# Requesting rows and up weights earlier in an expert stage, and moving a subtract from GpSimd to VectorE

## The chip, the cores and the metric

The kernel runs on one core of a Trainium2 chip. Its time is the device time of one execution in microseconds (us). A core has TensorE (PE, with its weight loads as PEld), VectorE (DVE), ScalarE (ACT), GpSimd (POOL) and SyncE (SP), which here only issues DMAs. Each engine runs its own instructions in order; they meet at semaphores.

## The reference, cut to what matters

Four layers of cross attention over 64 sequences of 64 tokens with 128 features. The change is in the last part of the last layer, a mixture of 8 experts in which each of 4096 tokens goes through its best two:

```python
h = _ln(x, ln_g, ln_b)
logits = h @ rw.T + rb
vals, idx = jax.lax.top_k(logits, K)            # K = 2 of E = 8
gates = jax.nn.softmax(vals, axis=-1)
h1 = gelu(einsum('nd,efd->enf', hf, fc1_w) + fc1_b)     # 128 -> 512, "up"
eo = einsum('enf,edf->end', h1, fc2_w) + fc2_b          # 512 -> 128, "down"
mixed = (gathered * gates_f[..., None]).sum(axis=1)
return x + mixed
```

## The kernel before, in words

The program is ten phases, and all five engines meet between them (`meet`, whose wait is line 223). The ninth phase, routing, writes every token's normalized row twice, once for each of its experts, into a table in HBM (`expert_rows`) in which each expert has its own region, and computes a plan: at which row each group starts and which expert it is. The tenth phase, the expert stage, is the one that changes. It works on NG = 23 groups of 512 rows. Group numbers are g or s; a pass is one turn of the loop on an engine.

What one group goes through:

- SyncE loads its rows (`load_rows`, 260 KB, line 1611), the expert's up weights (512 KB, line 1623), its bias (`e_bias`, 2.5 KB, line 1627) and its down weights (512 KB, line 1623). Row number and expert are read from the plan into a register by `value_load` ahead of the DMA. `rows_in` has RB = 6 buffers, so rows(g) wait until `moe_returned` says that group g-6 has landed; `w_up` and `w_down` have two each, so up(g) waits for the up products of group g-2 (`moe_h_done`) and down(g) for the down products of group g-2 (`moe_down_done`).
- TensorE transposes the rows (L1648), ScalarE reads them from PSUM twice (L1682 to `g_T`, L1684 rounded to `x_hi`, which is `sb_qT_hi`), and the rest, `x_lo = g_T - x_hi` (`sb_qT_lo`, `moe_x_split`), is made by GpSimd (L1732).
- TensorE makes four up products of three matmuls each (in `product_in_parts`, L1086), ScalarE applies Gelu (L1691), VectorE rounds to `h_hi` by a cast (L1715) and subtracts for `h_lo` (L1717).
- TensorE makes the down product, twelve matmuls (L1671), ScalarE adds the bias (L1705), TensorE transposes back (L1662), ScalarE scales the rows by the gate into `y_rows` (L1698, two buffers), and GpSimd scatters them to `expert_outs` in HBM with four indirect DMAs of 128 rows (L1739). Each group's four wait until all earlier ones have landed.

TensorE's pass s holds: transposes of group s+1, up products of s, transposes back of s-2, down product of s-1. It waits for `moe_up_loaded` and `moe_x_split` ahead of the up products. GpSimd's pass s holds the subtract of group s+1 and then the scatter of group s-2. `wait_alone` puts a wait on an instruction of its own (L77). When all groups have landed, SyncE loads the results back (L1633), VectorE adds them to X (L1724), and SyncE writes the output (L1637).

Of the kernel before, what the change touches and what calls it, by code (L numbers as in the profile page):

```python
# [34 lines left out]
P = 128  # L35
# [38 lines left out]
def wait_alone(e, sem, value):  # L74

    wait(e, sem, value)
    e.nop(nofuse=True)  # L77
# [34 lines left out]
def build(nc, a, out):  # L112
# [7 lines left out]
    with ctx:  # L120
# [61 lines left out]
        def col(name):  # L182
            at, n = COLS[name]
            return cols[:, at:at + n]
# [182 lines left out]
        def l0_pool(e, c):  # L367
            e.memset(half_power[:, :], -0.5)
            e.memset(zeros[:, :], 0.0)
            e.wait_ge(sem("params_loaded"), 16 * len(loads))  # L370
            for i in range(2):
                e.tensor_copy(twice[:, S * i:S * i + S], ident[0:S, 0:S])
            e.tensor_copy(ident_16[:, :], ident[:, :])
            e.tensor_copy(bv_wide[:, 0], col("sa_bv").to_broadcast([P, P]))
            e.tensor_copy(bv_wide[:, 1], col("ca_bv").to_broadcast([P, P])).then_inc(sem("bv_wide"), 1)
            e.tensor_tensor(bases[:, 0], row("ln11_b"), row("ca1_bo"), ALU.add)
            meet(e, 0)
            e.memset(rel_sb[:, :, 0:1], 0.0).then_inc(sem("l0_rel_pad"), 1)
            e.memset(blank[:, :, 0:D], 0.0)
            e.memset(blank[:, :, D + 1:ROW], 0.0)  # L380
            e.tensor_copy(blank[:, :, D:D + 1].bitcast(U32), ids[:, 2 * NT:].unsqueeze(2)).then_inc(sem("blank_ready"), 1)

            def fetch_expert(k):
                e.dma_start(e_raw[:, :], a["e_W"][bass.ds(k, 1)].rearrange("a p c -> p (a c)"))\
                    .then_inc(sem("expert_loaded"), 16)

            def split_expert(k):
# [12 lines left out]

            def step(k, u, head, front, back):
                if back:
                    (store_expert if u else fetch_expert)(k)
                if head:
                    m = 2 * k + u + 2
                    e.wait_ge(sem(f"l0_mask_loaded{u}"), 16 * (k + 2))
                    wait_alone(e, sem("l0_rows_done"), 4 * (m - 1))
                    e.tensor_scalar(mask_bias[:, u], mask8[:, u], MASKED, None, ALU.mult)\
                        .then_inc(sem("l0_mask_ready"), 1)
                if back:  # L410
                    n = 2 * k + u
                    x_inv_std_pool(e, "l0", n + 1, n, 1)
                if head:
                    m = 2 * k + u + 2
                    wait_alone(e, sem(f"l0_kv_loaded{u}"), 32 * (k + 2))
                    wait_alone(e, sem("l0_context_done"), 8 * (m - 1))
                    e.tensor_copy(kv_tok[:, u], kv_in[:, u]).then_inc(sem("l0_kv_kept"), 1)
                if back and u:
                    wait_alone(e, sem("expert_stored"), 16 * k + 16)
                elif back:  # L420
                    split_expert(k)
            walk(e, NT, step)

        def l0_tensor(e, c):
# [22 lines left out]
            for left, right in ((wqT, wkT), (wqT, rT), (pb_wide, rT), (wvT, wo0)):  # L447
                if left is wvT:
                    e.wait_ge(sem("l0_vo_loaded"), 32)
                for q in range(4):  # L450
# [2 lines left out]
                        h = 4 * q + i  # L453
                        ins = e.matmul(o[:, i * P:(i + 1) * P], left[:, h], right[:, h], start=True, stop=True)
                    ins.then_inc(sem("l0_table_done"), 1)
            e.wait_ge(sem("bv_wide"), 1)
            for i, n in enumerate(("sa", "ca")):
                ins = e.matmul(PS[:, 2, P * i:P * i + P], bv_wide[:, i], w_out[n][:, :], start=True, stop=True)
            ins.then_inc(sem("bases_done"), 1)
            meet(e, 0)  # L460

            def step(k, u, head, front, back):
# [87 lines left out]
        def l0_vector(e, c):  # L550
# [11 lines left out]
            for table in ("QK", "QR", "rel_bias", "VO"):  # L562
                for q in range(4):
# [9 lines left out]
                        ins = e.tensor_copy(to[:, 4 * q:4 * q + 4], product)  # L573
                    ins.then_inc(sem("l0_table_drained"), 1)
                    n += 1
            e.wait_ge(sem("bases_done"), 1)
            for i, bias in enumerate(("sa_bo", "ca_bo")):
                e.tensor_tensor(bases[:, 1 + i], PS[:, 2, P * i:P * i + P], row(bias), ALU.add)
            meet(e, 0)
# [1027 lines left out]
        def moe_sync(e, c):  # L1607
            def load_rows(s):
                wait_alone(e, sem("moe_returned"), 16 * QT * (s - RB + 1))
                r = e.value_load(plan[0:1, 0, s:s + 1], min_val=0, max_val=MAX_ROW)  # L1610
                e.dma_start(rows_in[:, s % RB], expert_rows[bass.ds(r, GROUP)].rearrange("(p t) c -> p t c", p=P))\
                    .then_inc(sem(f"moe_rows_loaded{s % 4}"), 16)
            load_rows(0)
            for s in range(NG):
                if s + 1 < NG:
                    load_rows(s + 1)
                x = e.value_load(plan[0:1, 1, s:s + 1], min_val=0, max_val=NE - 1)
                wait_alone(e, sem("moe_h_done"), FC * (s - 1))
                wait_alone(e, sem("moe_y_kept"), s - BB + 1)
                for i, to in ((0, w_up), (1, w_down)):  # L1620
                    if i:
                        wait_alone(e, sem("moe_down_done"), s - 1)
                    e.dma_start(to[:, s % 2].bitcast(F32).rearrange("p a c -> p (a c)"),
                                expert_halves[bass.ds(2 * x + i, 1)].rearrange("a p c -> p (a c)"))\
                        .then_inc(sem(f"moe_{('up', 'down')[i]}_loaded{s % 2}"), 16)
                    if not i:
                        e.dma_start(e_bias[:, s % BB], a["e_bias"][bass.ds(x, 1)].rearrange("a p c -> p (a c)"))\
                            .then_inc(sem(f"moe_up_loaded{s % 2}"), 16)
            e.wait_ge(sem("moe_returned"), 16 * QT * NG)
            e.wait_ge(sem("moe_down_done"), NG)  # L1630
            for j in range(4):
                for i in range(2):
                    e.dma_start(returned(i, j), expert_outs[bass.ds(i * NTOK + j * NTOK // 4, NTOK // 4)]  # L1633
                                .rearrange("(t p) d -> p t d", p=P)).then_inc(sem(f"moe_rows_loaded{j}"), 16)
            for j in range(4):
                e.wait_ge(sem("moe_mixed"), 2 * j + 2)
                e.dma_start(out.rearrange("(t b) s d -> (b s) t d", b=2)[:, NT // 4 * j:NT // 4 * (j + 1)],  # L1637
                            X[:, NT // 4 * j:NT // 4 * (j + 1)]).then_inc(sem("out_written"), 16)
# [67 lines left out]
                        .then_inc(sem("moe_y_kept"), 1)  # L1706

        def moe_vector(e, c):
            for s in range(NG):
                u = s % 2  # L1710
                if 0 <= s < NG:
                    wait(e, sem("moe_down_done"), s - 1)
                    for f in range(FC):
# [10 lines left out]
                    e.tensor_tensor(xs, xs, returned(i, j), ALU.add).then_inc(sem("moe_mixed"), 1)  # L1724

        def moe_pool(e, c):
            for s in range(-1, NG + 2):
                if s + 1 < NG:
                    g, v = s + 1, (s + 1) % 2
                    e.wait_ge(sem("moe_x_kept"), g + 1)  # L1730
                    wait(e, sem("moe_h_done"), FC * (g - 1))
                    e.tensor_tensor(x_lo[:, v], g_T[:, v], x_hi[:, v].bitcast(F32), ALU.subtract)\  # L1732
                        .then_inc(sem("moe_x_split"), 1)
                if 0 <= s - 2 < NG:
                    g = s - 2
                    e.wait_ge(sem("moe_y_ready"), g + 1)
                    wait_alone(e, sem("moe_returned"), 16 * QT * g)
                    for t in range(QT):
                        e.indirect_dma_start(  # L1739
                            out=expert_outs, out_offset=bass.IndirectOffsetOnAxis(  # L1740
                                ap=rows_in[:, g % RB, t, D:D + 1].bitcast(U32), axis=0),
                            in_=y_rows[:, g % 2, t], in_offset=None).then_inc(sem("moe_returned"), 16)

        L0 = dict(sync=l0_sync, gpsimd=l0_pool, tensor=l0_tensor, vector=l0_vector, scalar=l0_scalar)
        AT = dict(sync=att_sync, gpsimd=att_pool, tensor=att_tensor, vector=att_vector, scalar=att_scalar)
# [138 lines left out]
```

## Time and profile before

| what | value |
|---|---|
| time before, median of 3 runs | 2361.67 us (2355.17 to 2367.89) |
| the profiled execution, its own time | 2362.87 us |
| its span | 2361.0 us, 53547 instructions |
| busy: TensorE, VectorE, ScalarE, GpSimd | 1858.5, 1403.0, 1143.5, 852.5 us |
| expert stage | first DMA issued at 2150.18 us, last scatter issued at 2337.59 us |

The span goes from the first to the last instruction of the profiled execution; all clock times in this text count from its start. Busy times are sums over an engine's instructions, in which waits and the issue of plain DMAs don't count. Matmuls are pipelined, so that a busy TensorE is not one at its peak.

### The profile page before, as it was taken

Reading aid. Unit: us, or ns where it says so; the run is one execution under the profiler, and the core shown is the slowest. Engines: PE = TensorE matmul, PEld = TensorE weight load, DVE = VectorE, ACT = ScalarE, POOL = GpSimd, SP = SyncE. Lnnn points to the kernel's source line nnn. Section 1 sums busy time; section 2 is a strip of 40 time slices with the busy share of each in tenths; the row PEclk is TensorE's granted clock in tenths of the full one; section 3 lists DMA queues with packets and bytes.
Section 4 is the critical chain, followed back from the end, with each engine's and each line's share of the span. In section 5 each row is a group of like instructions: output and inputs, shape, how many; then the busy total and the mean of one; then the engine's idle time right before and its main releaser. Section 6 shows DMA issues by size and latency. Waiting matters only on the chain. (4 is left out here: it accounts for less than half of the span.)

```text
span 2361.0 us, 53547 instructions
## 1 busy us (share of the span) xinstructions
PE 1858.5 (79%) x15946; PEld 1394.0 (59%) x15946; DVE 1403.0 (59%) x4243; ACT 1143.5 (48%) x3419; POOL 852.5 (36%) x1414
## 2 busy tenths in 40 slices
PE   8898998998999877799789977538997886225993
PEld 7666666766767656566566656215665664224772
DVE  3455555545545546487667764786774785224874
ACT  0455455445445543355456643216774774003772
POOL 0112112111112214355456653343442443443774
PEclk6899999999999998899899989668996997556997
DMA  6544444554454530222100000000000000004775
GB/s 167 106 95 108 106 97 96 113 107 97 108 107 90 117 69 0 104 91 92 60 14 16 16 6 0 0 0 1 0 0 11 12 11 10 27 27 129 224 216 168
DMA packets 214228, 166.54 MB, mean 71 GB/s; under 512 B 27216, under 2 KB 188368, under 8 KB 213776
## 3 DMA queue, kind: packets, MB, share of 16 engines
q1 hardware_dynamic: 205584, 142.84, 24.6%
q0 software_dynamic: 8576, 22.88, 2.8%
q8 instruction: 32, 0.52, 0.1%
q14 instruction: 36, 0.29, 0.0%
HBM read 91.92 MB, written 73.76 MB: 70 GB/s over the span
## 5 line engine op out<-in xcount | busy, mean ns | idle before, releaser
L241 POOL TENSOR_SCALAR sb_next_var_eps<-sb_next_moments 128x1 f32<-128x1 f32 (+1 forms) x184 | 43.2, 235 | 697.0 <-DVE sb_next_moments L236 695.8
L634 DVE CUSTOM_DVE_ANT_0 sb_probs<-PS,sb_work 128x128 f32<-128x128 f32 x512 | 113.3, 287 | 303.2 <-DMA sb_work<-rel_scratch 302.1
L788 POOL TENSOR_TENSOR sb_work<-sb_work,sb_cols 128x512 f32<-128x512 f32 x128 | 134.1, 1048 | 318.4 <-ACT sb_work L995 203.4
L682 ACT ACTIVATE sb_probs<-sb_probs,sb_work 128x128 f32<-128x128 f32 x512 | 197.8, 388 | 100.0 <-DVE sb_work L640 100.0
L926 DVE TENSOR_REDUCE sb_work<-PS 128x8 f32<-128x512 f32 x256 | 175.5, 686 | 87.1 <-PE PS L831 85.9
L674 ACT ACTIVATE sb_work<-PS 128x512 f32<-128x512 f32 x128 | 76.4, 597 | 291.5 <-PE PS L532 291.5
L502 PE MATMUL PS<-sb_work,sb_tables 128*128 128x128 f32 x1024 | 143.8, 298 | 64.1 <-ACT sb_work L664 64.1
L809 PE MATMUL PS<-sb_ident,sb_work 128*128 128x128 f32 x1024 | 168.3, 289 | 32.5 <-ACT sb_work L962 27.6
L962 ACT ACTIVATE sb_work<-sb_work 128x512 f32<-128x512 f32 x256 | 161.3, 630 | 59.9 <-DVE sb_work L928 59.2
L928 DVE TENSOR_TENSOR sb_work<-PS,sb_work 128x512 f32<-128x512 f32 x256 | 177.1, 692 | 8.8
L502 PEld LDWEIGHTS PS<-sb_work,sb_tables 128*128 128x128 f32 x1024 | 134.8, 206 | 74.2 <-ACT sb_work L664 70.2
L809 PEld LDWEIGHTS PS<-sb_ident,sb_work 128*128 128x128 f32 x1024 | 116.5, 145 | 69.1 <-ACT sb_work L962 54.5
L852 PE MATMUL PS<-sb_v_ones,sb_work 128*64 128x18 f32 x4096 | 147.3, 215 | 3.8 <-ACT sb_work L968 3.7
L522 PE MATMUL PS<-sb_work 128*128 128x128 f32 x1024 | 149.6, 290 | 0.0
L852 PEld LDWEIGHTS PS<-sb_v_ones,sb_work 128*64 128x64 f32 x4096 | 134.8, 142 | 22.4 <-issue 10.2
L664 ACT ACTIVATE sb_work<-PS,sb_key_bias 128x128 f32<-128x128 f32 x512 | 138.8, 366 | 17.8 <-PE PS L502 17.8
L968 ACT ACTIVATE sb_work<-PS 128x512 f32<-128x512 f32 x256 | 139.8, 595 | 6.1 <-PE PS L809 2.6
L522 PEld LDWEIGHTS PS<-sb_work 128*128 128x128 f32 x1024 | 125.1, 193 | 29.2 <-issue 29.2
L538 PEld LDWEIGHTS PS<-sb_tables,sb_work 128*128 128x128 f32 x1024 | 116.7, 192 | 21.0 <-ACT sb_work L674 21.0
L538 PE MATMUL PS<-sb_tables,sb_work 128*128 128x128 f32 x1024 | 122.5, 278 | 0.0
L245 POOL TENSOR_TENSOR sb_tile_inv_std<-sb_next_var_eps,sb_half_power 128x1 f32 (+3 forms) x184 | 119.0, 647 | 8.7
L623 DVE COPY sb_probsT<-PS 128x512 f32<-128x512 f32 x128 | 84.1, 688 | 61.4 <-PE PS L494 60.4
(272 smaller groups left out, 4357.4 us busy)
## 6 DMA issues: line engine op xcount, KB each, us to landing
rel_scratch<-sb_work SPq DMA_DIRECT2D x64, 516.0 KB, 6.5
sb_work<-rel_scratch SPq DMA_DIRECT2D x64, 512.0 KB, 6.5
expert_rows<-sb_blank SPq DMA_DIRECT2D x36, 520.0 KB, 2.8
sb_w_up<-expert_halves SPq DMA_DIRECT2D x23, 512.0 KB
sb_w_down<-expert_halves SPq DMA_DIRECT2D x23, 512.0 KB
expert_halves<-sb_e_halves POOLq DMA_DIRECT2D x16, 512.0 KB, 8.2
sb_work<-expert_rows SPq DMA_DIRECT2D x23, 260.0 KB
sb_e_raw<-e_W POOLq DMA_DIRECT2D x16, 256.0 KB, 3.0
```

Of the source, the lines that this page charges most:

```text
L502: ins = e.matmul(PS[:, (shift + g) % 2, i * P:i * P + P], QK[:, 4 * g + i], kvT[:, v, 1], start=True, stop=True)
L522: ins = e.matmul(o[:, i * KL:i * KL + KL], qkT[:, b, h:h + 2], kvT[:, v, :, b], start=False, stop=(i == 3), skip_group_check=True)
L538: ins = e.matmul(o[:, 0:D], pkvT[:, h], VO[:, h], start=(h == 0), stop=(h == H - 1))
L664: ins = e.activation(qkT[:, :, h], PS[:, (shift + g) % 2, i * P:i * P + P] .rearrange("p (b q) -> p b q", b=2), ACT.Identity, bias=key_bia ...
L682: ins = e.activation(probs[:, v, b, hp], probs[:, v, b, hp], ACT.Exp, bias=neg_max[:, v, b, hp:hp + 1], scale=SCALE0, accum_out=row_sum[:, ...
L788: e.tensor_tensor(k_masked[:, u], k_sb[:, u].rearrange("p (b k) -> p b k", b=2).unsqueeze(2) .to_broadcast([P, 2, 4, S]), col("place").uns ...
L809: ins = e.transpose(PS[:, 4 + j, i * P:i * P + P], att_probs[:, u, 8 * j + 2 * i:8 * j + 2 * i + 2], ident[:, :])
L852: ins = e.matmul(values[S * b:S * b + S, 2 * i:2 * i + 2], att_probsT[:, i, S * b:S * b + S], v_ones[:, u, b, 2 * i:2 * i + 2], start=True ...
L926: e.tensor_reduce(top, mine, AX.X, ALU.max).then_inc(sem("att_max_ready"), 1)
L928: e.tensor_tensor(by_group(att_probs[:, v])[:, 2 * j:2 * j + 2], mine, top.unsqueeze(3).to_broadcast([P, 2, 4, S]), ALU.subtract)\
L962: e.activation(att_probs[:, v, 8 * j:8 * j + 8], att_probs[:, v, 8 * j:8 * j + 8], ACT.Exp, scale=c["scale"]).then_inc(sem("att_exp_done"), 1)
L968: e.activation(att_probsT[:, 4 * j:4 * j + 4].rearrange("p i q -> p (i q)"), PS[:, 4 + j], ACT.Copy)\
```

## The change

In SyncE's program of the expert stage the order of requests is another: rows are requested three groups ahead of the pass in which the loop stands, and up weights and bias one group. Down weights are requested one group ahead as well, in the last place. The waits in front of each request are those of before, with the number of the group adapted. The expert's number is now read from the plan twice for each group, once for up and once for down. The subtract `x_lo = g_T - x_hi` goes from GpSimd's program to VectorE's, where it stands ahead of the casts of the group before; GpSimd keeps the scatters and the wait ahead of each group of them. In the first phase two semaphores, `bv_wide` and `bases_done`, become one, `bases`.

```diff
-            e.tensor_copy(bv_wide[:, 1], ...).then_inc(sem("bv_wide"), 1)
+            e.tensor_copy(bv_wide[:, 1], ...).then_inc(sem("bases"), 1)
-            e.wait_ge(sem("bv_wide"), 1)
+            e.wait_ge(sem("bases"), 1)
-            ins.then_inc(sem("bases_done"), 1)
+            ins.then_inc(sem("bases"), 1)
-            e.wait_ge(sem("bases_done"), 1)
+            e.wait_ge(sem("bases"), 2)
...
+            def load_weights(s, i):
+                if i == 0:
+                    wait_alone(e, sem("moe_h_done"), FC * (s - 1))
+                    wait_alone(e, sem("moe_y_kept"), s - BB + 1)
+                else:
+                    wait_alone(e, sem("moe_down_done"), s - 1)
+                x = e.value_load(plan[0:1, 1, s:s + 1], min_val=0, max_val=NE - 1)
+                e.dma_start((w_up, w_down)[i][:, s % 2]..., expert_halves[bass.ds(2 * x + i, 1)]...)
+                    .then_inc(sem(f"moe_{('up', 'down')[i]}_loaded{s % 2}"), 16)
+                if i == 0:
+                    e.dma_start(e_bias[:, s % BB], a["e_bias"][bass.ds(x, 1)]...)
+                        .then_inc(sem(f"moe_up_loaded{s % 2}"), 16)
             load_rows(0)
+            load_weights(0, 0)
+            load_rows(1)
+            load_weights(0, 1)
+            load_rows(2)
             for s in range(NG):
                 if s + 1 < NG:
-                    load_rows(s + 1)
-                x = e.value_load(plan[0:1, 1, s:s + 1], min_val=0, max_val=NE - 1)
-                wait_alone(e, sem("moe_h_done"), FC * (s - 1))
-                wait_alone(e, sem("moe_y_kept"), s - BB + 1)
-                for i, to in ((0, w_up), (1, w_down)):
-                    if i:
-                        wait_alone(e, sem("moe_down_done"), s - 1)
-                    e.dma_start(...)            # up, bias, down of group s
+                    load_weights(s + 1, 0)
+                if s + 3 < NG:
+                    load_rows(s + 3)
+                if s + 1 < NG:
+                    load_weights(s + 1, 1)
...
         def moe_vector(e, c):
-            for s in range(NG):
+            for s in range(-1, NG):
                 u = s % 2
+                if s + 1 < NG:
+                    g, v = s + 1, (s + 1) % 2
+                    e.wait_ge(sem("moe_x_kept"), g + 1)
+                    wait(e, sem("moe_h_done"), FC * (g - 1))
+                    e.tensor_tensor(x_lo[:, v], g_T[:, v], x_hi[:, v].bitcast(F32), ALU.subtract)\
+                        .then_inc(sem("moe_x_split"), 1)
                 if 0 <= s < NG:
...
         def moe_pool(e, c):
-            for s in range(-1, NG + 2):
-                if s + 1 < NG:
-                    g, v = s + 1, (s + 1) % 2
-                    e.wait_ge(sem("moe_x_kept"), g + 1)
-                    wait(e, sem("moe_h_done"), FC * (g - 1))
-                    e.tensor_tensor(x_lo[:, v], g_T[:, v], x_hi[:, v].bitcast(F32), ALU.subtract)\
-                        .then_inc(sem("moe_x_split"), 1)
-                if 0 <= s - 2 < NG:
-                    g = s - 2
-                    e.wait_ge(sem("moe_y_ready"), g + 1)
-                    wait_alone(e, sem("moe_returned"), 16 * QT * g)
-                    ...
+            for g in range(NG):
+                e.wait_ge(sem("moe_y_ready"), g + 1)
+                wait_alone(e, sem("moe_returned"), 16 * QT * g)
+                for t in range(QT):
+                    e.indirect_dma_start(...)
```

## Rows read from the trace of the kernel before

**Rows 1.** Busy time by stretches, expert stage: us of PE, PEld, DVE, ACT, POOL; clock; DMA.

```profile
2175.00:2225.00 50.00, 47.06 (x229) 37.67 (x228) 42.73 (x60) 39.92 (x79) 37.06 (x35) 1.00 0.70 222
```

**Rows 2.** Timeline of TensorE, first up product of four passes [idle before, releaser].

```profile
2157.93 0.79 PE L1086 MATMUL PS<-sb_qT_hi,sb_w_up 128*128 128x512 f32 x1 [1.09 <-DMA sb_work<-e_bias]
...
2224.74 0.47 PE L1086 MATMUL PS<-sb_qT_hi,sb_w_up 128*128 128x512 f32 x1 [0.40 <-issue]
...
2232.35 0.47 PE L1086 MATMUL PS<-sb_qT_hi,sb_w_up 128*128 128x512 f32 x1 [0.95 <-DMA sb_work<-e_bias]
...
2312.70 0.47 PE L1086 MATMUL PS<-sb_qT_hi,sb_w_up 128*128 128x512 f32 x1 [0.81 <-issue]
```

**Rows 3.** Timeline of GpSimd: start us, us, line, operation.

```profile
2223.35 1.29 POOL L1732 TENSOR_TENSOR sb_qT_lo<-sb_work,sb_qT_hi 128x512 fp32r<-128x512 f32 x1
2225.49 1.03 POOL L1739 DMA_INDIRECT expert_outs<-sb_work  x1 [0.85 <-issue]
...
2229.47 1.48 POOL L1739 DMA_INDIRECT expert_outs<-sb_work  x1 [0.30 <-issue]
2230.97 1.28 POOL L1732 TENSOR_TENSOR sb_qT_lo<-sb_work,sb_qT_hi 128x512 fp32r<-128x512 f32 x1
2233.01 0.98 POOL L1739 DMA_INDIRECT expert_outs<-sb_work  x1 [0.76 <-issue]
...
2240.53 0.98 POOL L1739 DMA_INDIRECT expert_outs<-sb_work  x1 [1.26 <-issue]
```

**Rows 4.** Groups of instructions from 2175 to 2319 us: count, busy us, mean ns.

```profile
L1739 POOL DMA_INDIRECT expert_outs<-sb_work x80 | 82.0, 1026 | 39.4 <-issue 34.1 <-ACT sb_work L1698 3.8 <-PE PS L1086 1.5
...
L1732 POOL TENSOR_TENSOR sb_qT_lo<-sb_work,sb_qT_hi 128x512 fp32r<-128x512 f32 x19 | 24.5, 1287 | 0.4
```

**Rows 5.** Timeline of GpSimd, first scatter of groups 0, 21 and 22.

```profile
2175.14 1.45 POOL L1739 DMA_INDIRECT expert_outs<-sb_work  x1 [3.15 <-ACT sb_work L1698]
...
2327.06 0.96 POOL L1739 DMA_INDIRECT expert_outs<-sb_work  x1 [2.01 <-issue]
...
2333.80 0.96 POOL L1739 DMA_INDIRECT expert_outs<-sb_work  x1 [2.00 <-issue]
```

**Rows 6.** The chain that ended last, its step at the last scatter.

```profile
2337.59 2.22 DMA expert_outs<-sb_work
```

**Rows 7.** Timeline of ScalarE, the rescaled rows of group 8.

```profile
2228.37 1.13 ACT L1698 ACTIVATE sb_work<-PS,sb_work 128x128 f32<-128x128 f32 x4
```

**Rows 8.** Timeline of VectorE beside and behind GpSimd's subtract.

```profile
2223.01 1.92 DVE L1715 CAST sb_h_hi<-sb_work 128x512 fp32r<-128x512 f32 x1
2224.96 0.69 DVE L1717 TENSOR_TENSOR sb_h_lo<-sb_work,sb_h_hi 128x512 fp32r<-128x512 f32 x1
```

**Rows 9.** Waits of all engines, 2175 to 2319 us: total us, times, longest.

```profile
DVE sb_h_hi L1715 <- ACT sb_work L1691: 17.9, 18, 1.4
```

**Rows 10.** Waits of SyncE's queue, 2160 to 2330 us: total us, times, longest.

```profile
SPq L77 <- DMA expert_outs<-sb_work: 9.4, 17, 1.0
```

**Rows 11.** Timeline of SyncE's DMA issues, start of the stage and one pass.

```profile
2150.18 1.48 SPq L1611 DMA_DIRECT2D sb_work<-expert_rows  x2
2152.82 0.34 SPq L1623 DMA_DIRECT2D sb_w_up<-expert_halves  x1
...
2224.12 0.33 SPq L1623 DMA_DIRECT2D sb_w_down<-expert_halves  x1
2225.54 0.33 SPq L1611 DMA_DIRECT2D sb_work<-expert_rows  x1
2226.78 0.31 SPq L1623 DMA_DIRECT2D sb_w_up<-expert_halves  x1
```

**Rows 12.** Busy time by stretches of 1 us, the last two columns DMA share and GB/s.

```profile
2224.00:2225.00 1.00, 0.60 (x5) 0.40 (x3) 0.97 (x2) 1.00 (x2) 0.64 (x1) 1.00 0.04 12
...
2230.00:2231.00 1.00, 1.00 (x7) 0.78 (x6) 0.97 (x3) 0.00 (x0) 0.98 (x2) 1.00 0.20 78
...
2238.00:2239.00 1.00, 0.99 (x7) 0.62 (x5) 1.00 (x1) 0.41 (x1) 1.00 (x1) 1.00 0.53 186
```

More of the change, by code:

```diff
@@ L374, in l0_pool @@
             e.tensor_copy(bv_wide[:, 0], col("sa_bv").to_broadcast([P, P]))
-            e.tensor_copy(bv_wide[:, 1], col("ca_bv").to_broadcast([P, P])).then_inc(sem("bv_wide"), 1)
+            e.tensor_copy(bv_wide[:, 1], col("ca_bv").to_broadcast([P, P])).then_inc(sem("bases"), 1)
             e.tensor_tensor(bases[:, 0], row("ln11_b"), row("ca1_bo"), ALU.add)
@@ L1612, in load_rows @@
                     .then_inc(sem(f"moe_rows_loaded{s % 4}"), 16)
+            def load_weights(s, i):
[5 more added lines that the diff above has]
+                x = e.value_load(plan[0:1, 1, s:s + 1], min_val=0, max_val=NE - 1)
+                e.dma_start((w_up, w_down)[i][:, s % 2].bitcast(F32).rearrange("p a c -> p (a c)"),
+                            expert_halves[bass.ds(2 * x + i, 1)].rearrange("a p c -> p (a c)"))\
+                    .then_inc(sem(f"moe_{('up', 'down')[i]}_loaded{s % 2}"), 16)
+                if i == 0:
+                    e.dma_start(e_bias[:, s % BB], a["e_bias"][bass.ds(x, 1)].rearrange("a p c -> p (a c)"))\
+                        .then_inc(sem(f"moe_up_loaded{s % 2}"), 16)
             load_rows(0)
+            load_weights(0, 0)
+            load_rows(1)
+            load_weights(0, 1)
+            load_rows(2)
             for s in range(NG):
                 if s + 1 < NG:
-                    load_rows(s + 1)
-                x = e.value_load(plan[0:1, 1, s:s + 1], min_val=0, max_val=NE - 1)
-                wait_alone(e, sem("moe_h_done"), FC * (s - 1))
-                wait_alone(e, sem("moe_y_kept"), s - BB + 1)
-                for i, to in ((0, w_up), (1, w_down)):
-                    if i:
-                        wait_alone(e, sem("moe_down_done"), s - 1)
[L1623 to L1628, printed above, removed]
+                    load_weights(s + 1, 0)
[3 more added lines that the diff above has]
+                    load_weights(s + 1, 1)
             e.wait_ge(sem("moe_returned"), 16 * QT * NG)
@@ L1726, in moe_pool @@
         def moe_pool(e, c):
-            for s in range(-1, NG + 2):
-                if s + 1 < NG:
-                    g, v = s + 1, (s + 1) % 2
-                    e.wait_ge(sem("moe_x_kept"), g + 1)
-                    wait(e, sem("moe_h_done"), FC * (g - 1))
-                    e.tensor_tensor(x_lo[:, v], g_T[:, v], x_hi[:, v].bitcast(F32), ALU.subtract)\
-                        .then_inc(sem("moe_x_split"), 1)
-                if 0 <= s - 2 < NG:
-                    g = s - 2
-                    e.wait_ge(sem("moe_y_ready"), g + 1)
-                    wait_alone(e, sem("moe_returned"), 16 * QT * g)
[L1738 to L1742, printed above, removed]
+            for g in range(NG):
+                e.wait_ge(sem("moe_y_ready"), g + 1)
+                wait_alone(e, sem("moe_returned"), 16 * QT * g)
+                for t in range(QT):
+                    e.indirect_dma_start(
+                        out=expert_outs, out_offset=bass.IndirectOffsetOnAxis(
+                            ap=rows_in[:, g % RB, t, D:D + 1].bitcast(U32), axis=0),
+                        in_=y_rows[:, g % 2, t], in_offset=None).then_inc(sem("moe_returned"), 16)
         L0 = dict(sync=l0_sync, gpsimd=l0_pool, tensor=l0_tensor, vector=l0_vector, scalar=l0_scalar)
```

## The prediction

> **What bounds the kernel now.** I read the busy time by stretches first. In the expert stage no engine is at its limit over 50 us: GpSimd counts 37.06 us, and TensorE 47.06 us with modelled ends [rows 1]. So I looked for a period instead. A pass is one turn of the stage's loop; by the first up product of each pass TensorE goes from 2224.74 to 2232.35 (7.61 us) there, and on to 2312.70 for pass 22, 11 passes at 7.31 us [rows 2]. Its idle time ahead of that product is 0.40, 0.95 and 0.81 us [rows 2]. The 7.61 us pass without its 0.95 us is 6.66 us: TensorE's own pass.
>
> The row calls that wait "e_bias". I don't believe it: the subtract on GpSimd (L1732) starts at 2223.35 and 2230.97 and takes 1.29 and 1.28 us [rows 3], so it ends at 2224.64 and 2232.25, and TensorE starts 0.10 us later both times. TensorE waits for the second part of the rows.
>
> Why is that subtract late? It takes 1.29 us, 19 times in this stretch [rows 4]. GpSimd starts it 0.02 us after the fourth scatter of a group (2229.47 plus 1.48 is 2230.95) [rows 3]. So the next question is the cycle of the scatters. It runs from the first one at 2175.14 to group 22's at 2333.80, 22 cycles in 158.66 us, 7.21 us each [rows 5]. One cycle is four indirect DMAs of 1.026 us [rows 4] with three steps of 0.30 us between them, 5.00 us, and then a gap of 2.21 us. The reader is to see in [rows 3] that the gap has the subtract in it, 0.85 and 0.76 us of wait behind it; and in [rows 5] that the gap is 2.00 us at the end of the stage as well, where no subtract is left. The gap is the wait for moe_returned: the last scatter lands 2.22 us after its issue [rows 6], which is 1.26 us after its 0.96 us end, and about 0.74 us more pass until GpSimd issues again. The subtract (0.02 plus 1.29 us) fits into those 1.26 us almost exactly. Nor does the scatter wait for data: ScalarE starts the rescaled rows of group 8 at 2228.37 and ends them 1.13 us later, at 2229.50 [rows 7], and their scatter starts at 2233.01 [rows 3], 3.5 us after.
>
> So the bound is GpSimd's scatter loop: issue four, wait until they have landed, issue again. TensorE, with 6.66 us, follows it.
>
> **The change part by part.**
>
> Subtract off GpSimd. 23 subtracts of 1.29 us leave GpSimd, 29.7 us. I cost this at nothing: the landing wait hides them, and without them it stands bare. If instead the cover were not there, each cycle would save what the subtract puts beyond landing; the unloaded gap with one (1.31 us and 0.76 us behind it, 2.07 us) against 2.00 without bounds that at 0.1 us a cycle, 2 us in all. With the floor in everything (four scatters of 0.96 us, 0.90 us, 2.00 us: 6.74 us, as 2327.06 to 2333.80 shows [rows 5]) the cycle could save 0.47 us, 10.3 us over 22. Nothing of this change can bring it under 6.74 us, since the wait between groups stays in moe_pool.
>
> Subtract onto VectorE. The nearest row is VectorE's own subtract of that form and size, 0.69 us [rows 8]. The moved one stands ahead of the four casts of a group, and needs ScalarE's x_hi, which comes ahead of the first Gelu of the group in ScalarE's order. VectorE waits for that Gelu anyway, 17.9 us in 18 passes, 1.0 us each [rows 9], and the 0.69 us fall into this wait; without it they would push the casts by 0.69 us. Queued behind it are those casts, and behind them next pass's down products, which have over 3 us. In return VectorE loses the stalls beside GpSimd's subtract: a cast took 1.92 us [rows 8] around 2223.35, when a plain one is under the 0.69 us subtract. So VectorE gains over 0.5 us a group, and that is off the path: cost nothing, gain nothing. TensorE no longer waits for GpSimd directly. It then runs ahead at 6.66 us until something else holds it: y_rows has two buffers, and rows_in six, whose reuse waits on the same moe_returned.
>
> Some of the scatters are long, 1.48 us [rows 3] against 0.96. That one ends as a VectorE pair and the subtract collide. The average excess is 5.00 less 4.74, 0.26 us a cycle. Bounds: all goes (minus 5.7 us over 22), or it doubles, since VectorE works on where it was held before (plus 5.7 us). I take a fifth of it, minus 1.2 us, nearer to no change because most of that excess can't come from a subtract that starts when the scatters are over.
>
> Here the Trainium skill has a rule against the change. "SBUF — State Buffer", section "SBUF: two separate sides", says that descriptors of a DMA issued from GpSimd can't be written while VectorE runs an operation in a two-port mode, and that whoever comes first holds the pair for the whole instruction. The rows agree only in part: VectorE makes four casts a group all through, yet the scatters' mean is only 0.07 us over 0.96 [rows 4, 5]. By the row the sum is minus 1.2 us, as above; by the page in full it is that of case (c) below.
>
> Order on SyncE. Before: rows(s+1), up(s), down(s). After: up(s+1), rows(s+3), down(s+1). Written as one stream, up and down alternate as before with the same waits: up(g) still needs the up products of group g-2, since w_up has two buffers. Only the rows move: from behind down(s) to behind up(s+1) and one group on. And rows(g) needs group g-6 landed in both. Today that is what SyncE waits for, 17 times, 9.4 us [rows 10]; rows go at 2225.54, when scatter 2225.49 shows that the landing has just come. That landing comes a little after the end of pass, which let down go at 2224.12 [rows 11]. So "three groups in advance" isn't to be had in the steady state: the rows' request leaves at the same event. What is new is that down stands behind that wait, by some 2.5 us (1.4 us, and 1.1 us for one more load of a register and issue, as between rows at 2225.54 and up at 2226.78, 1.24 us). Down has over a pass in hand: it is used behind the ups, 3 us into the pass after next. Up now has down's 512 KB shortly ahead of it. Today traffic is dry again 4.6 us after the landing (share 0.20 at 2230 [rows 12]). After, rows, down and up, 1284 KB, all start after the landing: at the stage's 222 GB/s [rows 1] 5.8 us, plus some 2 us of issue, 7.8 us. How much is allowed? Landing(g), then up(g+5), pass g+5, its rescaled rows 4.8 us in (2224.74 to 2229.50), and scatter(g+3), which is due at landing(g+2): two cycles less 4.8, 9.6 us. 1.8 us in hand: cost nothing.
>
> Traffic in the landing window. Ahead of the scatter of 2225.49 the share is 0.04 at 2224 [rows 12], and GpSimd waits 0.85 us behind the subtract; ahead of that of 2240.53 the share is 0.53 at 2238, and it waits 1.26 us [rows 3]. The mean gap is 2.21 us against 2.00 at rest. The later, denser requests can lengthen it: bounds minus 0.21 and plus 0.5 us a cycle (minus 4.6, plus 11 us). I take zero, as the same bytes stay in flight beside it today.
>
> Start of the stage. Rows(0) are issued at 2150.18, up(0) at 2152.82, and TensorE's first up product waits 1.09 us for it until 2157.93 [rows 2, 11]. Up(0) now leaves ahead of rows(1), about 1.1 to 1.5 us earlier; rows(1), also needed ahead of that product, leaves as much later. Bounds minus 1.1 and plus 1; I take minus 0.8 us. The renamed semaphore "bases" moves nothing.
>
> Sum on the profiled execution: 2361.0 minus 1.2 minus 0.8 is 2359.0; with the 1.9 us around the span (2362.87 less 2361.0) 2360.9. The median of the runs shown is 2361.67, 1.2 us under that execution: 2359.7 us.
>
> **The rivals.** The forecast, scatter loop still the bound at 7.0 to 7.4 us: 2356 to 2365 us, chance 0.62.
> (a) The loop falls to its floor of 6.74 us, as the subtract and its collisions were all that was over it: 2361.67 less 10.3 less 0.8, 2350.5 us. For it: the tail's rows. Against: traffic stays in the window. 0.16.
> (b) Up weights arrive late: landing to up takes 11 us in place of 7.8, and the period becomes half of 11 plus 4.8, 7.9 us, plus 15 us over 22: 2376 us. It decides from 9.6 us on; at 10.3 us it is 7.55, plus 7.5 us. For it: down is now ahead of up behind a wait; against: the 1.8 us. 0.12 in all, 0.04 for over 0.5%.
> (c) This is the other side: VectorE, no longer held, stretches all four scatters to the 1.48 us seen once. Cycle 5.92 plus 0.90 plus 2.21, 9.03 us, plus 40 us: 2402 us. It gives over 0.5% from 1.16 us a scatter on; casts run beside them today at 1.03. 0.04.
> (d) The edit does nothing at all, 2361.7 us, as loop and start are as before: 0.06.
>
> **How the numbers follow.** A measurement of this kernel tells about 0.5%, 12 us, from no change: faster is under 2350, slower over 2373. Case (a) ends just inside; noise and a larger gain at the start carry 0.06 over. Slower: 0.04 of (b) and 0.03 of (c), 0.07. Same 0.87. The range goes from (a) to the milder half of (b), 2350 to 2367.
>
> **What would show it.** Right: the gap between the fourth scatter of a group and the next stays at 2.0 to 2.7 us with nothing in it; first scatter of group 0 to group 22 stays near 22 times 7.1; TensorE still idles some 0.4 us a pass, now named up weights or ScalarE behind moe_returned; rows are requested right at a landing, down directly behind; casts on VectorE fall to one length. Wrong: a gap of under 2 us, a pass of 6.7 us all through (a), up products that idle over 1 us behind w_up (b), scatters over 1.1 us on the mean (c).

## The result: 1.2% slower, and the profile after

The changed kernel takes 2389.66 us in the median of 4 runs (2385.41 to 2395.17), the kernel before 2359.39 us beside it; the ratio is 1.0125 with a 95% interval of 1.0085 to 1.0165. The forecast was 2359.7 us, no change, in a range of 2350 to 2367 us.

In the profiled executions the span grows by 22.7 us, from 2361.0 to 2383.7 us. GpSimd's first scatter of group 0 and of group 22, from its timeline, show where:

```profile
2171.06 1.34 POOL L1748 DMA_INDIRECT expert_outs<-sb_work  x1 [31.60 <-ACT sb_work L1709]
...
2356.66 0.95 POOL L1748 DMA_INDIRECT expert_outs<-sb_work  x1 [2.01 <-issue]
```

That is 185.60 us for 22 cycles, 8.44 us each, against 158.66 us and 7.21 us [rows 5]: 26.9 us lost. The first scatter comes 4.1 us earlier; the stage's first request, the next row, from SyncE's timeline, stands 2.8 us earlier, in work that the edit doesn't touch, and the way from it to the first scatter takes 23.70 us in place of 24.96.

```profile
2147.36 0.34 SPq L1611 DMA_DIRECT2D sb_work<-expert_rows  x1
```

Now one cycle. First GpSimd's timeline, then SyncE's, then TensorE's first up product of two passes:

```profile
2206.39 0.96 POOL L1748 DMA_INDIRECT expert_outs<-sb_work  x1 [3.49 <-DMA expert_outs<-sb_work]
2207.66 0.96 POOL L1748 DMA_INDIRECT expert_outs<-sb_work  x1 [0.30 <-issue]
2208.92 1.48 POOL L1748 DMA_INDIRECT expert_outs<-sb_work  x1 [0.30 <-issue]
2210.71 1.10 POOL L1748 DMA_INDIRECT expert_outs<-sb_work  x1 [0.30 <-issue]
2215.09 0.95 POOL L1748 DMA_INDIRECT expert_outs<-sb_work  x1 [3.29 <-issue]
```

```profile
2206.43 0.33 SPq L1611 DMA_DIRECT2D sb_work<-expert_rows  x1
2207.60 0.47 SPq L1622 DMA_DIRECT2D sb_w_down<-expert_halves  x1
2208.96 0.33 SPq L1622 DMA_DIRECT2D sb_w_up<-expert_halves  x1
...
2215.13 0.33 SPq L1611 DMA_DIRECT2D sb_work<-expert_rows  x1
```

```profile
2205.37 0.50 PE L1086 MATMUL PS<-sb_qT_hi,sb_w_up 128*128 128x512 f32 x1 [1.53 <-DMA sb_work<-e_bias]
...
2214.24 0.50 PE L1086 MATMUL PS<-sb_qT_hi,sb_w_up 128*128 128x512 f32 x1 [2.22 <-DMA sb_work<-e_bias]
```

The gap, from the end of the fourth scatter (2211.81) to the next group's first, is 3.28 us, with nothing on GpSimd in it; before it was 2.0 to 2.6 us [rows 3]. Rows leave right at a landing, as forecast, down 1.2 us behind them (before: ahead of them [rows 11]) and up 2.5 us behind. And the landing that GpSimd waits for comes when the loads are through. The busy time in stretches of 1 us (the last two columns are the DMA share and GB/s) has them in flight into the stretch that ends at 2214 (share 0.26), and nothing behind it:

```profile
2211.00:2212.00 1.00, 1.00 (x7) 0.65 (x5) 0.69 (x1) 0.39 (x1) 0.80 (x1) 1.00 0.81 295
2212.00:2213.00 1.00, 0.01 (x1) 0.00 (x0) 0.00 (x0) 1.00 (x3) 0.00 (x0) 1.00 0.72 260
2213.00:2214.00 1.00, 0.00 (x0) 0.00 (x0) 0.33 (x1) 0.64 (x1) 0.00 (x0) 1.00 0.26 91
2214.00:2215.00 1.00, 0.77 (x3) 0.67 (x4) 0.36 (x1) 0.00 (x0) 0.00 (x0) 1.00 0.00 0
```

TensorE starts at 2214.24, when up is there; the landing is at about 2214.35 (2215.09 less the 0.74 us of the prediction). Before, traffic was down to a share of 0.04 ahead of such a landing [rows 12]. SyncE's wait for landings, 17 times as before, grows from 9.4 [rows 10] to 80.1 us, and it now stands in front of both weights (SyncE's waits from 2160 to 2330 us):

```profile
SPq L77 <- DMA expert_outs<-sb_work: 80.1, 17, 5.3
```

The scatters themselves hardly change; their row from 2175 to 2319 us has a mean of 1.059 us against 1.026 [rows 4]:

```profile
L1748 POOL DMA_INDIRECT expert_outs<-sb_work x65 | 68.8, 1059 | 73.7 <-issue 38.5 <-DMA expert_outs<-sb_work 34.6 <-ACT sb_work L1709 0.6
```

Of GpSimd's 73.7 us of idle time in that row only 0.6 us are a wait for ScalarE's rows: the data is there, the landing isn't.

### The profile page after: what moved, and what is told of

It reads as the page before. It is cut to its first block and busy times, and to the rows that moved or that the text cites. A ratio compares the mean times of both kernels' runs of the same rounds, so it can differ in the third digit from the quotient of the medians.

```text
span 2383.7 us, 53615 instructions
## 1 busy us (share of the span) xinstructions
PE 1866.6 (78%) x15946; PEld 1400.4 (59%) x15946; DVE 1389.6 (58%) x4266; ACT 1145.2 (48%) x3419; POOL 822.5 (35%) x1391
## 5 line engine op out<-in xcount | busy, mean ns | idle before, releaser
L1748 POOL DMA_INDIRECT expert_outs<-sb_work x92 | 95.3, 1036 | 126.6 <-issue 54.3
```

## The experiments

The table has each kernel's scatter cycle from group 0 to 18, and of it the four scatters with their three steps (mean of groups 0 to 17) and the gap (mean of groups 1 to 18), all from GpSimd's timeline of its profiled execution; then the ratio of its time to that of the kernel before, which ran beside it. The cycle is that of one execution, the ratio is over 4 to 10 of each kernel.

| kernel | cycle us | four scatters us | gap us | ratio, 95% interval |
|---|---|---|---|---|
| before | 7.29 | 5.02 | 2.27 | 1 |
| changed | 8.80 | 5.14 | 3.66 | 1.0125, 1.0085 to 1.0165 |
| 1 subtract only | 8.64 | 5.31 | 3.33 | 1.0060, 1.0035 to 1.0086 |
| 2 order only | 8.93 | 5.26 | 3.67 | 1.0126, 1.0073 to 1.0178 |
| 3 rows last | 8.25 | 5.28 | 2.96 | 1.0040, 1.0010 to 1.0069 |
| 4 eight row buffers | 7.82 | 5.38 | 2.44 | 1.0021, 0.9997 to 1.0045 |
| 5 no bytes for down | 7.53 | 5.09 | 2.45 | 1.0008, 0.9987 to 1.0029 |
| 6 eight buffers, no cast | 7.70 | 5.29 | 2.42 | 1.0019, 1.0001 to 1.0036 |
| 7 down behind scatter | 7.68 | 5.23 | 2.45 | 1.0096, 1.0067 to 1.0125 |
| 8 before, extra load | 9.81 | 5.12 | 4.69 | 1.0185, 1.0148 to 1.0222 |
| 9 pace restored | 7.58 | 5.17 | 2.41 | 1.0014, 1.0004 to 1.0025 |
| 10 changed, no landing wait | 7.55 | 4.92 | 2.63 | 1.0005, 0.9989 to 1.0022 |
| 11 before, no landing wait | 6.89 | 5.08 | 1.81 | 0.9943, 0.9923 to 0.9962 |
| 12 eight buffers, no landing wait | 6.77 | 5.04 | 1.73 | 0.9929, 0.9902 to 0.9957 |

**1 and 2: each half alone.** The first keeps `moe_sync` of before, the second the subtract in `moe_pool`:

```diff
 # 1: the changed kernel with
-                    load_weights(s + 1, 0) ... load_rows(s + 3) ... load_weights(s + 1, 1)
+                    load_rows(s + 1) ... up(s), bias(s), down(s), as before
 # 2: the kernel before with the changed moe_sync
```

> The changed kernel with SyncE's order of before; only the subtract is on VectorE. Traffic theory (the scatters land late because down and up weights are both requested right behind a landing, so that their 1 MB is in flight when the next group's scatters end): the order is what costs, so the scatter cycle is back at 7.0 to 7.3 us and the time at 0.995 to 1.002 of before. VectorE theory (VectorE, no longer held by GpSimd's subtract, slows the scatters): the cycle stays near 8.4 us and the time at about 1.012.

> The kernel before with SyncE's new order; the subtract stays on GpSimd. Traffic theory: the gap from the fourth scatter to the next group's first is 3 to 4.5 us as in the changed kernel, the cycle 8.7 to 9 us in groups 1 to 18, the time 1.010 to 1.016 of before. VectorE theory: as before, 1.00.

The second behaves like the changed kernel, as the traffic theory wants. The first doesn't: with the old order and the subtract on VectorE the gap is 3.33 us, too. Of its 1.35 us more a cycle, 1.06 us are gap and only 0.29 us slower scatters, so the VectorE theory doesn't get its share either. Each half alone brings the long gaps, and the two together are no worse. Its time, 1.0060, lies between the two expectations and fits neither. The traffic theory needed something that the subtract does.

**3 and 4: down freed from the wait.** Two ways to let down leave without a landing:

```diff
 # 3
                 if s + 1 < NG:
                     load_weights(s + 1, 0)
+                    load_weights(s + 1, 1)
                 if s + 3 < NG:
                     load_rows(s + 3)
-                if s + 1 < NG:
-                    load_weights(s + 1, 1)
 # 4
-        RB, BB = 6, 4
+        RB, BB = 8, 4
```

> The changed kernel with two requests swapped: in each pass up, down, rows in place of up, rows, down, so that down weights don't stand behind the rows' wait for a landing. Traffic theory: down leaves at the end of a pass again, 1.5 us or more ahead of the landing, the gap is back at 2.0 to 2.7 us, the time 0.995 to 1.002 of before. Theory that it is the distance of the rows (three groups) or the second load of the expert's number: 1.01.

> The changed kernel with 8 buffers for rows in place of 6. The rows' request then waits for a landing two groups earlier and doesn't hold down and up. Traffic theory: requests leave as TensorE's passes end, the gap is 2.0 to 2.9 us, the cycle 6.9 to 7.4 us, the time 0.993 to 1.003 of before. If the order of the queue costs by itself, whatever it waits for: 1.01.

The third falls between its two expectations, with a mean gap of 2.96 us and 1.0040: it mixes cycles of 7.4 and 9.6 us. Two neighbours of one timeline, GpSimd's, then SyncE's, show what decides:

```profile
2185.53 0.96 POOL L1748 DMA_INDIRECT expert_outs<-sb_work  x1 [0.30 <-issue]
2188.49 1.31 POOL L1748 DMA_INDIRECT expert_outs<-sb_work  x1 [2.00 <-issue]
...
2192.81 1.48 POOL L1748 DMA_INDIRECT expert_outs<-sb_work  x1 [0.30 <-issue]
2198.09 1.27 POOL L1748 DMA_INDIRECT expert_outs<-sb_work  x1 [3.81 <-issue]
```

```profile
2186.97 0.33 SPq L1622 DMA_DIRECT2D sb_w_down<-expert_halves  x1
...
2189.75 0.33 SPq L1622 DMA_DIRECT2D sb_w_up<-expert_halves  x1
...
2193.78 0.33 SPq L1622 DMA_DIRECT2D sb_w_down<-expert_halves  x1
```

The first group's last scatter ends at 2186.49 and down is requested 0.48 us later: gap 2.00 us. The next one's ends at 2194.29, and down was requested 0.51 us earlier: 3.80 us. I took this over groups 1 to 17 of eight kernels, those of before, changed, and runs 1 to 4, 6 and 7, by the time from the last request for 512 KB of weights to the end of the fourth scatter:

| request ahead of the end | cycles | gap us |
|---|---|---|
| under 0.3 us | 7 | 2.00 to 2.14 |
| 0.3 to 2.9 us | 53 | 52 of them over 3.0, median 3.8 |
| 2.9 to 3.3 us | 9 | 2.21 to 3.54 |
| over 3.3 us | 67 | 66 of them under 3.0, median 2.02 |

I read this as follows: a scatter lands only behind a load of weights that was requested ahead of it and is still unfinished. The traces show the requests and the gaps, and not in what order the DMA engines finish them. The fourth kernel meets its expectation in the gap and in the time, but its mean cycle, 7.82 us, is over the 7.4 us expected. It settles by group 6, with down requested 5.7 us and up 6.6 us behind the first scatter, both behind the last one's end (5.39 us) and without a long gap from then on; what is left there is the length of the scatters: 7.39 us a cycle where 6.74 us [rows 5] is the floor. Three of its early gaps are long (3.95, 3.46 and 5.47 us). Three rows of GpSimd's timeline in the steady part:

```profile
2262.57 1.43 POOL L1748 DMA_INDIRECT expert_outs<-sb_work  x1 [0.30 <-issue]
2264.30 1.14 POOL L1748 DMA_INDIRECT expert_outs<-sb_work  x1 [0.30 <-issue]
2267.54 0.96 POOL L1748 DMA_INDIRECT expert_outs<-sb_work  x1 [2.09 <-issue]
```

**5 and 8: traffic taken away, traffic added.** The fifth leaves out the down weights of all groups but the first two, so its result is not the model's. The eighth has the one semaphore `bases` of the changed kernel, as do runs 9 and 11.

```diff
 # 5: the changed kernel with
+                if i and s > 1:
+                    e.dma_start(w_down[:, s % 2, 0, 0:8].bitcast(F32),
+                                expert_halves[bass.ds(2 * x + i, 1), :, 0:8]...)...
+                    return
 # 8: the kernel before with, behind the bias,
+                        wait_alone(e, sem("extra_loaded"), 16 * s)
+                        e.dma_start(extra, expert_halves[bass.ds(2 * x, 1)]...)\
+                            .then_inc(sem("extra_loaded"), 16)
```

> The changed kernel, whose down weights are loaded whole for the first two groups only; after them each down request carries 4 KB (32 bytes a partition) in place of 512 KB, so the work of later experts is left out of the result. Order, waits, number of requests and all engines' work stay. Traffic theory: 0.5 MB less is in flight when the scatters end; the loads behind a landing are dry about 1.5 us earlier, about 6 us behind it, the gap falls from 3.7 to 2.0 to 2.6 us and the cycle from 8.8 to 7.2 to 7.7 us, the span by 20 to 30 us. If waits or the order alone cost: no change, 1.012 of before.

> The kernel before with 512 KB more to load for each group, right behind the bias, into a buffer that nothing reads. Subtract on GpSimd and all orders stay. Traffic theory: the loads behind a landing are dry at about 6.3 us in place of 4.6, later than the scatters' end at 4.9, so the gap grows from 2.27 to 3.2 to 4 us, the cycle to 8.2 to 9 us and the time to 1.008 to 1.016 of before. If scatters land on their own account: gap and time as before.

Both go the way of the traffic theory. With 0.5 MB less, and the same requests at the same places, the changed kernel's gap falls from 3.66 to 2.45 us and its span from 2383.7 to 2363.5 us. GpSimd's and SyncE's timelines of one cycle:

```profile
2252.24 0.96 POOL L1753 DMA_INDIRECT expert_outs<-sb_work  x1 [0.30 <-ACT sb_work L1714]
2255.56 0.95 POOL L1753 DMA_INDIRECT expert_outs<-sb_work  x1 [2.37 <-issue]
```

```profile
2250.89 0.33 SPq L1627 DMA_DIRECT2D sb_w_up<-expert_halves  x1
```

Here 512 KB of up weights are requested 2.3 us ahead of the scatters' end (2253.20), inside the second row of the table above, and the gap is only 2.36 us. In groups 1 to 17 up leaves 1.9 to 3.0 us ahead in 16 cycles, and 15 of these have gaps of 2.00 to 2.79 us, one of 3.44. So it isn't the time of the last request that decides but what is unfinished with it: the table holds for kernels in which down is loaded as well.

With 0.5 MB more the kernel before loses 2.5 us a cycle, more than the 0.9 to 1.7 us that I expected, and ends at 1.0185, over my range. GpSimd's and SyncE's timelines of one cycle of it:

```profile
2275.77 0.96 POOL L1743 DMA_INDIRECT expert_outs<-sb_work  x1 [0.30 <-DMA expert_outs<-sb_work]
2276.75 1.28 POOL L1736 TENSOR_TENSOR sb_qT_lo<-sb_work,sb_qT_hi 128x512 fp32r<-128x512 f32 x1
2282.21 1.13 POOL L1743 DMA_INDIRECT expert_outs<-sb_work  x1 [4.18 <-issue]
```

```profile
2274.06 0.33 SPq L1631 DMA_DIRECT2D sb_work<-expert_halves  x1
2276.29 0.33 SPq L1624 DMA_DIRECT2D sb_w_down<-expert_halves  x1
```

The extra load goes out 2.7 us and down 0.4 us ahead of the scatters' end (2276.73), and the gap is 5.5 us: here both loads are in front of the landing.

**6: the cast.** The scatters' length was the other loss in the fourth kernel, and the cast the suspect.

```diff
 # 6: the fourth kernel with
-                        e.tensor_copy(h_hi[:, u, f], h_full[:, f])
+                        e.tensor_tensor(h_hi[:, u, f], h_full[:, f], zeros[:, 0:1].to_broadcast([P, QT * P]), ALU.add)
```

> The kernel with 8 row buffers, in which VectorE makes its rounded copy by adding a zero (a tensor_tensor) in place of the cast. With 8 buffers the gap is 2.00 us in groups 6 to 17, but four scatters take 5.39 us against 4.74 at rest. Port theory: the cast is what slows GpSimd's scatters; without it four scatters take 4.74 to 4.85 us, the cycle is 6.75 to 6.9 us, the time 0.990 to 0.998 of before, though VectorE has about 1 us more work a group. If it isn't the cast: scatters stay at 5.39 us and the time at 1.002 or more.

The port theory fails in this form. Without a single cast in the stage four scatters still take 5.32 us. VectorE's timeline and, under it, GpSimd's:

```profile
2260.96 0.69 DVE L1732 TENSOR_TENSOR sb_h_hi<-sb_work,sb_zeros 128x512 fp32r<-128x512 f32 x1
2261.69 0.69 DVE L1734 TENSOR_TENSOR sb_h_lo<-sb_work,sb_h_hi 128x512 fp32r<-128x512 f32 x1
```

```profile
2262.14 1.07 POOL L1748 DMA_INDIRECT expert_outs<-sb_work  x1 [0.30 <-issue]
```

Work of VectorE goes with the stretching, cast or not: in the 14 traces 315 scatters overlap no instruction of VectorE, and none of them takes over 0.99 us; 973 overlap one, and 447 of these take over 1.00 us, up to 1.50. That is an association over all traces and no test of its own, and which property of an instruction does it stays open.

**7 and 9: the phase put right.** In the kernel before TensorE waits for GpSimd's subtract, which follows the scatters. A pass then ends, and down goes out, behind the last scatter [rows 3, 11]. Run 7 makes down wait for the scatters, run 9 gives TensorE its old wait back while VectorE keeps the real subtract:

```diff
 # 7: the first kernel with, in moe_pool and moe_sync,
+                e.nop(nofuse=True).then_inc(sem("moe_scattered"), 1)      # behind the four scatters
+                        wait_alone(e, sem("moe_scattered"), s - 3)        # ahead of down(s)
 # 9: the first kernel with, in moe_pool ahead of the scatters, and in moe_tensor
+                    e.tensor_tensor(spare[:, v], x_hi[:, v]..., x_hi[:, v]..., ALU.subtract)\
+                        .then_inc(sem("moe_paced"), 1)
+                    e.wait_ge(sem("moe_paced"), s + 1)
```

> Subtract on VectorE and SyncE's order of before, as in the first experiment (1.006, cycles of 7.4 and 9 us mixed), and one wait more: down(g) is requested only when GpSimd has issued the scatters of group g-4. The first experiment's long cycles are those in which down went out ahead of the last scatter. Traffic theory: no such cycle is left, the gap is 2.0 to 2.6 us in all groups, the cycle 7.2 to 7.6 us, the time 0.998 to 1.004 of before. If the phase of down and scatter doesn't matter: 1.006 or more, as one more wait only costs.

> Subtract on VectorE and SyncE's order of before (first experiment: 1.006), and GpSimd gets a subtract of the same size back, in the old place, on numbers that nothing uses; TensorE waits for it ahead of its up products, as it did before. Pace theory (the subtract held TensorE so that a pass ended, and down was requested, only behind the last scatter): the gap is back at 2.0 to 2.7 us in all groups, down at 5.6 to 5.9 us behind the first scatter, the cycle 7.1 to 7.5 us, the time 0.998 to 1.003. If VectorE's extra subtract is what costs: 1.006 or more, since GpSimd has more work as well.

Run 9 is as the pace theory said: GpSimd has its dummy to do, VectorE its extra subtract, and the time is back within 0.14% of before, against 0.60% in run 1. Its cycle, 7.58 us, is a little over the range, with scatters of 5.17 us against 5.02. GpSimd's and SyncE's timelines:

```profile
2226.49 0.96 POOL L1748 DMA_INDIRECT expert_outs<-sb_work  x1 [0.30 <-ACT sb_work L1700]
2227.48 1.05 POOL L1741 TENSOR_TENSOR sb_work<-sb_qT_hi 128x512 f32<-128x512 f32 x1
2229.69 0.98 POOL L1748 DMA_INDIRECT expert_outs<-sb_work  x1 [1.16 <-issue]
```

```profile
2228.05 0.33 SPq L1624 DMA_DIRECT2D sb_w_down<-expert_halves  x1
```

Down goes out 0.6 us behind the last scatter's end. Two early cycles of run 9 don't fit into the table above: in groups 1 and 2 down leaves only 0.02 and 0.24 us ahead of the end, and the gaps are 3.35 and 2.97 us. Run 7 missed its expectation: 1.0096 is over the 0.998 to 1.004 of the traffic theory, and on the side named for a phase that doesn't matter. Its profiled execution (2368.72 us, the fastest of its five) has 15 of 18 cycles at 7.1 to 7.75 us and one of 8.54 us at the start, but also two of 9.16 us, in which down left 0.37 and 1.45 us ahead of the scatters' end all the same. I take it that there the passes had moved on against the scatters, so that a wait for the group four back was too little. The other runs go up to 2390.6 us; I have no profile of those. So the phase theory rests on run 9 and on the cycles of the traces, not on run 7's time.

**10 to 12: the landing out of the cycle.**

```diff
 # 10: the changed kernel, 11: the kernel before, 12: the fourth kernel, each with
-                wait_alone(e, sem("moe_returned"), 16 * QT * g)              # ahead of the scatters of g
+                if g >= 20:
+                    wait_alone(e, sem(f"moe_returned{(g - 1) % 2}"), 16 * QT * ((g - 1) // 2 + 1))
-                            ... .then_inc(sem("moe_returned"), 16)
+                            ... .then_inc(sem(f"moe_returned{g % 2}"), 16)
```

The waits of SyncE for a row buffer and of ScalarE for `y_rows` name the semaphore of that group's parity. Groups 20 to 22 keep their wait, since padding rows of neighbouring groups are written to one region of `expert_outs`; with other inputs such neighbours can come earlier, and a kernel for use needs a second region.

> The changed kernel, in which GpSimd doesn't wait for the landing of a group ahead of the next group's scatters; two semaphores by the parity of the group guard the buffers. Groups 20 to 22 keep the wait. Traffic theory: scatters still land late, but the landing is no longer in GpSimd's cycle; rows, down and up still leave behind a landing, three groups later: 7.0 to 7.5 us a group, the time 0.993 to 1.002 of before. If the loads themselves set the pace (bandwidth): the cycle stays at 8.8 and the time at 1.012.

> The kernel before without the same wait (groups 20 to 22 keep it), order and subtract as before, the two semaphores of the first phase merged to make room. The scatter loop of 7.2 us falls away; TensorE's own pass of 6.66 us is next: cycle 6.7 to 6.9 us, the time 0.992 to 0.997 of before. If something else holds 7.2 us: 1.00.

> The changed kernel with 8 row buffers and without the wait for a landing between groups (groups 20 to 22 keep it). Neither a landing nor GpSimd's work is in TensorE's way: cycle 6.65 to 6.8 us, the time 0.990 to 0.996 of before. If the request order or VectorE's subtract costs on TensorE's own path: 7.0 us or more and 0.998 or more.

All three as expected by the traffic theory (the tenth's cycle is 0.05 us over). The changed kernel without this one wait is level with before, at 1.0005. But it isn't level with the kernel before without the same wait: 7.55 us a cycle against 6.89, and 1.0005 against 0.9943. So of the 1.51 us a cycle that the change cost 0.66 us are left when GpSimd no longer waits for landings. Two waits of run 10, GpSimd's from 2175 to 2319 us and SyncE's from 2160 to 2330 us (total us, times, longest), show where:

```profile
POOL expert_outs L1751 <- ACT sb_work L1711: 48.8, 19, 5.8
SPq L77 <- DMA expert_outs<-sb_work: 54.3, 17, 4.9
```

GpSimd now waits for ScalarE's rows. SyncE still waits 54.3 us for landings, to get a row buffer back (2.9 us in run 11), with down and up behind that wait. Run 12 takes this wait away too, by eight buffers, keeps the new order and the subtract on VectorE, and is at 6.77 us. So the late landing cost by two paths: GpSimd's own wait, and SyncE's wait ahead of the weights.

The eleventh shows that the scatter loop was the bound of the kernel before: 7.29 us become 6.89, next to TensorE's 6.66. The twelfth beats both kernels, 0.9929 of before (2352.95 us in the median against 2368.31 beside it). In GpSimd's timeline its scatters now start behind ScalarE's rows and not behind a landing:

```profile
2241.73 1.18 POOL L1751 DMA_INDIRECT expert_outs<-sb_work  x1 [1.68 <-ACT sb_work L1711]
...
2245.73 1.12 POOL L1751 DMA_INDIRECT expert_outs<-sb_work  x1 [0.30 <-issue]
2248.59 1.12 POOL L1751 DMA_INDIRECT expert_outs<-sb_work  x1 [1.74 <-ACT sb_work L1711]
```

## Why the prediction was wrong, step by step

- **The bound**: right. TensorE waited for the subtract, the subtract for the scatters, these for a landing. Run 11 confirms it.
- **Order on SyncE**: right in place and size. Rows leave at the same event as before, down is behind it, and up is usable 7.8 us behind the rows' request (2206.43 to 2214.24), the 7.8 us of the sum. But "cost nothing" held only for a landing that is on time: between runs 10 and 11 this wait in front of the weights is what is left, 0.66 us a cycle. The sign named for case (b) came about too, with 25.2 us of TensorE's waits ahead of its up products in 15 passes, up to 2.8 us each (2175 to 2319 us). In the changed kernel that didn't set the cycle, as GpSimd waited for landings and only 0.6 us for ScalarE's rows.
- **Traffic in the landing window**: the step that failed. It took zero, "as the same bytes stay in flight beside it today", with plus 0.5 us a cycle as the bound. Measured is plus 1.39 us (2.27 to 3.66). What counts is not how many bytes a cycle has but how many are requested ahead of the last scatter and unfinished; [rows 12] had shown that window nearly empty in the good case, and I used the spread of good cases, 2.0 to 2.6 us, as if it bounded a full one. Case (b) has this place too, with up late and TensorE idle, but it let the landing come on time, so that it gave only half of the delay to the cycle. Here landing, requests, loads and the next landing form one ring: 1.2 and 1.4 us of issue, the loads, then the scatter behind them.
- **Subtract off GpSimd**: also wrong. It does cost GpSimd nothing, but TensorE's wait for it was named as the thing that falls away, and what that wait did was not asked. It kept the end of a pass, and so down's request, behind the scatters. Run 1 lost 1.35 us a cycle without it, run 9 got 1.06 of them back.
- **Subtract onto VectorE**: the sum took minus 0.05 us a cycle for scatters; measured is plus 0.12 in the changed kernel and plus 0.29 in run 1. The sign was wrong, the size stayed inside the bounds. Case (c), 1.48 us for each scatter, didn't come about: 1.059 us. VectorE did gain as forecast: its casts have a mean of 0.467 us against 0.730 before (2175 to 2319 us).
- **Start of the stage**: minus 1.26 us, forecast minus 0.8.

The sum with the measured terms: 1.51 us (8.80 less 7.29) over 18 cycles is 27.3 us, less 1.3 us at the start, less the 2.8 us ahead of the stage, 23.2 us; the spans differ by 22.7. The 2.8 us are no part of the change: the stage's first request lies between 2140.4 and 2153.7 us in the 14 profiled executions. For the same reason one span can't be set against another closely, and the loss is read from the cycles.

On the rule that I weighed, another section of the Trainium skill's page "SBUF — State Buffer", "Who interferes with whom", tells more. It says that a tensor_tensor has no two-port mode, and infers that it doesn't disturb the writing of descriptors; but it also says that one with both inputs in SBUF contends with reads of SBUF by GpSimd. With tensor_tensor alone on VectorE, run 6 has 5.32 us for four scatters against 4.74 at rest. So either that inference doesn't hold for these scatters or they read SBUF as they are issued, which no run separates.

The Trainium skill's "DMA: Bandwidth & Descriptors", section "SWDGE vs HWDGE vs iDMA", says that DMAs of GpSimd and of SyncE feed different internal queues of a DMA engine, which serves them in turn. An estimate from that rule: 64 KB of scatter should lose about its own length beside a load, some 0.2 us at 347 GB/s, the rate from 2343 to 2344 us in the trace of the kernel before; the table under runs 3 and 4 has 1.8 us (a median of 3.8 against 2.0), which is nearer to the 1.5 us that 512 KB take. The measurement decides here. By what mechanism the scatter is held back, in the queues or at the memory, no run shows.

## What to carry to other kernels

When a wait on a helper engine is taken away, ask what was timed by it: a slow instruction can be the one that keeps two streams of DMAs apart. In a loop that waits for its own small DMAs to land, put large loads behind the last of them or so far ahead that they are finished by then, or take the landing out of the loop by a semaphore for each buffer. And when a gap varies with traffic, price it by the full window, not by the spread of the good case.

## What the runs showed of the hardware that I had not expected

- A group of four indirect DMAs of 64 KB each lands 1.26 us behind its end on a quiet queue, and mostly 1.4 to 2.4 us later when a load of 512 KB was requested 0.3 to 2.9 us ahead of that end, in kernels that load up and down for each group. Without down (run 5) a request for 512 KB 1.9 to 3.0 us ahead costs 0 to 0.8 us in 15 of 16 cycles.
- The edge can be sharp; in run 3, 0.48 us behind the end costs nothing (2.00 us), 0.51 us ahead of it costs 1.8 us (3.80 us).
- Two engines that wait for each other through DMAs can fall into different patterns in one run: run 3 mixes cycles of 7.0 to 7.6 us and of 8.5 to 9.7 us, with all instructions equal.
